# Tables of the means' turns read from SBUF, and their comparisons moved among the additions

## The reference

```python
# layer 0: messages weighted by an MLP of the edge attributes, summed at each src node
h = jax.nn.silu(edge_rbf @ W1 + b1)
aggregated = jax.ops.segment_sum(node_feats[col] * (h @ W2 + b2), row, num_segments=n_nodes)
x = _layernorm(x + (jnp.concatenate([node_feats @ Wself + bself, aggregated], -1) @ Wcat + bcat))
# layer 1: means over the neighbours in both directions, then a GRU cell
a_in  = _seg_mean((h @ W_in.T + b_in)[src], dst, N)
a_out = _seg_mean((h @ W_out.T + b_out)[dst], src, N)
x = _layernorm(x + _gru_cell(jnp.concatenate((a_in, a_out), 1), h, w_ih, w_hh, b_ih, b_hh))
```

## Time and profile before

| what | value |
|---|---|
| time, median of 3 runs | 7878.73 us (7873.51 to 7900.0) |
| profiled execution, its own time | 7875.48 us |
| its span, first to last instruction | 7873.8 us |
| busy share: PE, DVE, ACT, POOL | 57%, 56%, 11%, 63% |
| mean granted clock of PE | 0.708 of full |
| stage of the means, first to last addition | 3290.5 to 7527.1 us |

### The profile page before, as it was taken

One profiled execution on the slowest core, in us unless ns is written; L12 is line 12 of the kernel. 1 busy time (PEld: TensorE's weight loads), 2 busy tenths in 40 slices (PEclk: granted clock), 3 DMA queues, 4 the chain that ended last, 5 costly groups with the idle time before them and its releaser, 6 DMA issues.

```text
span 7873.8 us, 126494 instructions
## 1 busy us (share of the span) xinstructions
PE 4516.3 (57%) x27084; PEld 3894.4 (49%) x27084; DVE 4432.0 (56%) x16895; ACT 841.4 (11%) x1997; POOL 4968.8 (63%) x5292
## 2 busy tenths in 40 slices
PE   4999999999997888433333333332333333333378
PEld 3777877777777886333333323232232332332344
DVE  7666666666668883444444544445444544444455
ACT  1222222222220001000000000000000000000023
POOL 1777777777772110477777777777577777777710
PEclk7778778777878995566666666666666666666689
DMA  2333333333336772222222222222122222222222
GB/s 91 111 111 112 110 112 111 112 109 112 110 107 217 225 221 67 69 51 54 53 53 53 51 53 53 53 53 52 37 53 53 50 53 53 53 53 53 53 64 74
DMA packets 872793, 657.16 MB, mean 83 GB/s; under 512 B 564443, under 2 KB 760144, under 8 KB 872064
## 3 DMA queue, kind: packets, MB, share of 16 engines
q0 software_dynamic: 163968, 348.11, 15.1%
q1 hardware_dynamic: 641797, 242.70, 13.1%
q10 hardware_dynamic: 66944, 65.50, 2.7%
HBM read 504.82 MB, written 138.16 MB: 82 GB/s over the span
## 4 chain that ended last, share of the span: by engine, by line
PE 21%; DVEq 15%; DVE 14%; POOL 9%; issue 9%; DMA 1%; ACT 0%; POOLq 0%; SPq 0%; ACTq 0%
DVEq L350 12%; POOL arena L657 9%; PE bank L1668 8%; PE bank L1620 6%; DVE acc_a L1347 5%; DVE acc_b L1347 5%; DVE arena L1336 3%; DVEq L1347 2%; PE bank L1712 1%; DVEq L1336 1%; PE bank L1649 1%; PE bank L1713 1%; PE bank L1714 1%; PE bank L1639 1%; PE bank L1647 1%
## 5 line engine op out<-in xcount | busy, mean ns | idle before, releaser
L657 POOL DMA_INDIRECT arena<-x1d,edge x3328 | 3190.7, 959 | 1086.6 <-issue 1006.3
L1668 PE MATMUL bank<-arena 128*128 x7040 | 1314.0, 370 | 2874.8 <-DVE arena L1336 2786.8
L1668 PEld LDWEIGHTS bank<-arena 128*128 128x128 f32 x7040 | 1269.0, 283 | 2920.0 <-issue 2920.0
L618 POOL DMA_INDIRECT msgs<-arena x1664 | 1646.4, 989 | 716.3 <-issue 495.6
L1336 DVE TENSOR_SCALAR arena<-iota_row,arena,edge 128x128 f32<-128x128 f32 x3520 | 935.9, 365 | 1287.0 <-issue 1282.9
L1347 DVE TENSOR_TENSOR acc_a<-acc_a,bank 128x129 f32 x1760 | 510.3, 290 | 463.2 <-PE bank L1668 240.9
L1347 DVE TENSOR_TENSOR acc_b<-acc_b,bank 128x129 f32 x1760 | 510.3, 290 | 438.9 <-PE bank L1668 219.7
L1592 PE MATMUL bank<-arena 128*128 (+1 forms) x3328 | 618.3, 343 | 0.0
L1560 PE MATMUL bank<-arena 64*128 64x128 f32 x3328 | 606.8, 336 | 0.4 <-ACT arena L723 0.4
L1568 PE MATMUL bank<-w2s,acc_b 128*128 128x128 f32 x3328 | 581.8, 328 | 0.0
L1620 PE MATMUL bank<-arena 128*128 128x128 f32 x3712 | 504.5, 301 | 94.3 <-DVE arena L1173 94.1
(11 more groups left out here) (275 smaller groups left out, 4197.2 us busy)
## 6 DMA issues: line engine op xcount, KB each, us to landing
arena<-rows SPq DMA_DIRECT2D x208, 512.0 KB
arena<-msgs SPq DMA_DIRECT2D x464, 136.0 KB, 3.0
arena<-msgs ACTq DMA_DIRECT2D x464, 136.0 KB, 3.2
arena<-x1d,edge POOLq DMA_INDIRECT x3328, 2.5
msgs<-arena POOLq DMA_INDIRECT x1664
arena<-xwin SPq DMA_DIRECT2D x208, 64.0 KB
arena<-acc_a SPq DMA_DIRECT2D x28, 448.0 KB, 4.7
arena<-in_edge_attr_dram SPq DMA_DIRECT2D x207, 32.0 KB
```

The source lines that it names most:

```text
L618: pool.indirect_dma_start(msgs, bass.IndirectOffsetOnAxis(ap=pos[:, b, j:j + 1], axis=0), mrow[:, b, j, :], None).then_inc(scattered[b], 16)
L657: pool.indirect_dma_start(grow_t[:, sl, 0:D], None, x1d, bass.IndirectOffsetOnAxis(ap=edge2[:, odd * RING + sl, 1:2].bitcast(i32), axis=0) ...
L1668: last = mm(bank[q % 2 * 4 + k // 2][:, (k % 2) * 256:(k % 2) * 256 + CW], oh1[:, q % 2, k, :], grow[:, bass.ds(rows_at[q * TG + k], CW)], ...
```

## The change

The tables of the turns are still written to DRAM. SP now copies each turn's 32 values (128 bytes) into one of two slots in SBUF (`turntab`, in the memory of `tprod`, which the messages' stage used), when DVE has made the first comparisons of the turn that comes two turns earlier. DVE waits for the slot and loads its registers from there. SP's list loads are placed between these copies; in half 1 the first copy comes after the first 16 lists, of which the last eight come after the second table has landed.

On DVE a turn makes the eight comparisons of group 0; then, for each of the eight passes, one comparison of group 1 followed by one addition of group 0, the first addition waiting for PE's group 0; then it waits for PE's group 1 and adds eight. The loop over turns has two turns in its body. Two semaphores are merged into others (`w1_in` into `xcopy`, `dstq_in` into `count_in`, with the waits raised to match).

```diff
+        turntab = tprod[:, :, :].rearrange("p a b -> p (a b)")[0:1, 0:4 * NT].bitcast(i32).rearrange("p (s k) -> p s k", s=2)
...
+        turn_in = [sem(f"turn_in{i}") for i in range(2)]
...
@@ SP, lists and tables @@
-            for b in range(ahead, GL):
-                need(sp, s["sum1_ready"], max(2 * b - 17, 0))
-                list_load(0, b)
+            def turn_load(half, it):
+
+                first = half * V1 // TG + it * (NT // TG)
+                need(sp, s["oh1_ready"], first - 2 * (NT // TG) + 1)
+                sp.dma_start(turntab[:, it % 2, :], sumtab[half:half + 1, it, :]).then_inc(turn_in[it % 2], 16)
+
+            for it in range(IT1):
+                turn_load(0, it)
+                b = it + ahead - 10
+                if ahead <= b < GL:
+                    sp.wait_ge(s["sum1_ready"], 2 * b - 17)
+                    list_load(0, b)
             sp.wait_ge(s["dst_sorted"], 1)
-            for b in range(GL):
-                sp.wait_ge(s["sum1_ready"], min(191 + 2 * b, V1 // TG) if b < ahead else V1 // TG + 2 * b - 17)
+            for b in range(ahead):
+                sp.wait_ge(s["sum1_ready"], min(191 + 2 * b, V1 // TG))
                 if b == ahead // 2:
                     pair_table(1)
+                    for i in range(2):
+                        sp.wait_ge(pair_copied[i], 2 * 64 * (CHUNKS // 2))
                 list_load(1, b)
+            for it in range(IT1):
+                turn_load(1, it)
+                b = it + ahead - 10
+                if ahead <= b < GL:
+                    sp.wait_ge(s["sum1_ready"], V1 // TG + 2 * b - 17)
+                    list_load(1, b)
@@ DVE, one turn @@
-            def sums1(half, it, lists):
+            def sums1(half, it, lists, slot, loads, start=False):
...
-                regs, of = load_table(dve, "dve_sum", 2 * NT, sumtab[half:half + 1, bass.ds(it, 1), :].rearrange("o t k -> o (t k)"), [NB * CW] * NT + [2 * LISTS - 2] * NT)
+                dve.wait_ge(turn_in[slot], 16 * loads)
+                dve.nop(nofuse=True)
+                regs, of = load_table(dve, "dve_sum", 2 * NT, turntab[:, slot, :], [NB * CW] * NT + [2 * LISTS - 2] * NT)
...
-                def onehots1(q):
-                    need(dve, s["sum1_ready"], first + q - 1)
+                def onehot1(q, k):
+                    return v.tensor_scalar(oh1[:, q % 2, k, :], iota_row[:, :], blk1[:, bass.ds(it * NT + q * TG + k, 1)], edge2_f[:, bass.ds(key_at[q * TG + k], 1)], ALU.add, ALU.is_equal)
+
+                if half or not start:
+                    dve.wait_ge(s["sum1_ready"], first - 1)
+                for k in range(TG):
+                    last = onehot1(0, k)
+                last.then_inc(s["oh1_ready"], 1)
+                for q in range(turn):
+                    more = q < turn - 1
+                    if more and (half or not start):
+                        dve.wait_ge(s["sum1_ready"], first + q)
                     for k in range(TG):
-                        last = v.tensor_scalar(oh1[:, q % 2, k, :], iota_row[:, :], blk1[:, bass.ds(it * NT + q * TG + k, 1)], edge2_f[:, bass.ds(key_at[q * TG + k], 1)], ALU.add, ALU.is_equal)
-                    last.then_inc(s["oh1_ready"], 1)
-
-                onehots1(0)
-                for q in range(turn):
-                    if q < turn - 1:
-                        onehots1(q + 1)
-                    dve.wait_ge(s["sum1_ready"], first + q + 1)
-                    for k in range(TG):
-                        need(dve, s["add1_done"], v0 + it * NT + q * TG + k)
+                        if more:
+                            last = onehot1(q + 1, k)
+                            if k == TG - 1:
+                                last.then_inc(s["oh1_ready"], 1)
+                        if k == 0:
+                            dve.wait_ge(s["sum1_ready"], first + q + 1)
+                        if k or q or half or not start:
+                            dve.wait_ge(s["add1_done"], v0 + it * NT + q * TG + k)
                         a = acc[:, bass.ds(at[q * TG + k], CW)]
                         v.tensor_tensor(a, a, bank[q % 2 * 4 + k // 2][:, (k % 2) * 256:(k % 2) * 256 + CW], ALU.add).then_inc(s["add1_done"], 1)
@@ DVE, the loop of turns: two turns in a body @@
-                with dve.Fori(max(a, 1), min(b, GL)) as it:
-                    sums1(half, it, it + half * GL + 1)
+                with dve.Fori(max(a // 2, 1), min(b, GL) // 2) as c:
+                    for i in range(2):
+                        sums1(half, 2 * c + i, 2 * c + i + half * GL + 1, i, c + lead)
...
```

More of the change, by code:

```diff
@@ L306, in gnn_kernel @@
         g_out g_stats g_moments u_added u_moments u_kept g_mv u_inv g_inv aux_split xcopy pool_step gather_own upd_step
-        grow_ones tiles_in lists_in list_in dstq_in pair_sums pair_out count_in slow_total slow_start w1_in slow_pool lotab_out reg_done wide_in digits_read local_ready slow_blocks slow_counted
+        grow_ones tiles_in lists_in list_in pair_sums pair_out count_in slow_total slow_start  slow_pool lotab_out reg_done wide_in digits_read local_ready slow_blocks slow_counted
         slow_hist rows_float columns_ready columns_read blk0_copied totals_in totals_out base_in""".split()
@@ L376, in _ @@
             for j in range(TG):
-                sp.dma_start(w1pad[j * A:(j + 1) * A, j, :], W1).then_inc(s["w1_in"], 16)
+                sp.dma_start(w1pad[j * A:(j + 1) * A, j, :], W1).then_inc(s["xcopy"], 16)
             sp.wait_ge(s["prep_out"], 1)
@@ L397, in _ @@
             sp.wait_ge(s["lotab_out"], 48)
-            sp.wait_ge(s["xcopy"], 32)
+            sp.wait_ge(s["xcopy"], 16 * (2 + TG))
             sp.wait_ge(s["flag_ready"], 1)
@@ L518, in _ @@
                 sp.wait_ge(pair_copied[i], 64 * (CHUNKS // 2))
-            sp.dma_start(dst_q[0:EQ, 0:EC], dst.rearrange("(p c) -> p c", c=EC)).then_inc(s["dstq_in"], 16)
-            for b in range(ahead, GL):
-                need(sp, s["sum1_ready"], max(2 * b - 17, 0))
-                list_load(0, b)
+            sp.dma_start(dst_q[0:EQ, 0:EC], dst.rearrange("(p c) -> p c", c=EC)).then_inc(s["count_in"], 16)
+            def turn_load(half, it):
[8 more added lines that the diff above has]
+                    list_load(0, b)
             sp.wait_ge(s["dst_sorted"], 1)
-            for b in range(GL):
-                sp.wait_ge(s["sum1_ready"], min(191 + 2 * b, V1 // TG) if b < ahead else V1 // TG + 2 * b - 17)
+            for b in range(ahead):
+                sp.wait_ge(s["sum1_ready"], min(191 + 2 * b, V1 // TG))
                 if b == ahead // 2:
                     pair_table(1)
+                    for i in range(2):
+                        sp.wait_ge(pair_copied[i], 2 * 64 * (CHUNKS // 2))
                 list_load(1, b)
+            for it in range(IT1):
[4 more added lines that the diff above has]
+                    list_load(1, b)
             mean_rows = [a[:, 0:NB * CW].rearrange("p (n c) -> p n c", c=CW) for a in (acc_a, acc_b)]
@@ L988, in _ @@
             dve.wait_ge(s["lotab_out"], 48)
-            dve.wait_ge(s["xcopy"], 32)
+            dve.wait_ge(s["xcopy"], 16 * (2 + TG))
             cnt, start = kcol[0:NB, 0:1], kcol[0:NB, 2:3]
@@ L1361, in turns @@
             def turns(half, a, b):
+                lead = half * IT1 // 2 + 1
                 if a == 0:
-                    sums1(half, 0, half * GL + 1)
-                with dve.Fori(max(a, 1), min(b, GL)) as it:
-                    sums1(half, it, it + half * GL + 1)
+                    for i in range(2):
+                        sums1(half, i, i + half * GL + 1, i, lead, start=(i == 0))
+                with dve.Fori(max(a // 2, 1), min(b, GL) // 2) as c:
+                    for i in range(2):
+                        sums1(half, 2 * c + i, 2 * c + i + half * GL + 1, i, c + lead)
                 if b == IT1:
-                    with dve.Fori(GL, IT1) as it:
-                        sums1(half, it, half * GL + GL)
+                    with dve.Fori(GL // 2, IT1 // 2) as c:
+                        for i in range(2):
+                            sums1(half, 2 * c + i, half * GL + GL, i, c + lead)
             pair_table(0)
@@ L1372, in _ @@
             turns(0, 0, ITH)
-            dve.wait_ge(s["dstq_in"], 16)
+            dve.wait_ge(s["count_in"], 32)
             for c, shift, mask in ((0, 7 + LO.bit_length() - 1, None), (1, 7, LO - 1)):
@@ L1600, in _ @@
             pe.wait_ge(s["prepared"], 1)
-            pe.wait_ge(s["w1_in"], 16 * TG)
+            pe.wait_ge(s["xcopy"], 16 * (2 + TG))
             pe.wait_ge(s["aux_in"], 16 * 6)
```

## The result

The changed kernel takes 8053.82 us (median of 4 runs, 8049.06 to 8064.51) against 7885.47 us of the kernel before beside it: a ratio of 1.022, interval 1.0203 to 1.0236. It is slower, as forecast (8072 us). The profiled execution took 8064.51 us with a span of 8062.9.

What follows compares the result with a forecast made beforehand. A serial DVE-PE ring of 18.79 us a turn bounds, POOL nearly as slow. Turns +198, start of half 1 +14, start of half 0 -5, gather waits -10: +197 us on 7875.48, 8072 us; range 7860 to 8290.

Steps and rivals of the forecast that it cites:

- ring of links: DVE's serial chain with PE in one turn of the means stage: 19.69 us forecast against 18.79 before.
- Table load: DVE's idle time at a turn's start: 2.65 us from the slot instead of 5.87, 3.22 us saved per turn.
- Mixing: Additions of group 0 alternating with comparisons of group 1 on DVE: 0.47 us a pair, between 0.42 and 0.69.
- second rival: Mixing on DVE hides nothing: a pair costs 0.69 us, 1.32 us more per turn, 8360 us; chance 0.10.
- Second group: PE's second eight passes, now waited for by DVE: 3.92 us per turn, at the 1.2 GHz clock level.
- first rival: PE's second group runs at full clock: turn 17.94 us, POOL bounds, 7825 us, 0.6% faster; chance 0.10.
- The queue's order: DVE takes its queue strictly in order, so seven ready comparisons stand behind the wait for PE's first group.
- third rival: Written order does not bind DVE; comparisons run under PE as before: turn 15.57 us, POOL bounds, 7825 us; chance 0.03.
- start of half 1: First slot of the second half is requested only after eight lists on SP, so DVE starts later: +14 us.
- start of half 0: First load of 9.44 us becomes a landing of 2.2 us and a load of 2.1 us: -5 us.
- waits for late gathers (-10): Turns where PE's second group and DVE waited for a gather find POOL ahead: three such waits, -10 us.
- One sign: A mark to look for in the profile after: POOL waiting for PE for over 200 us in total.

Runs made afterwards that it cites:

- the ring alone: Kernel before, with tables loaded from the SBUF slots but all sixteen comparisons still ahead of the additions: 7830.15 us, ratio 0.9936.

## Why the prediction was right

The mechanism was the forecast one, and its ring of links holds link by link:

| link of a turn | predicted | measured, mean |
|---|---|---|
| idle time ahead of the comparisons | 2.65 | 2.52 |
| eight comparisons to PE's start | 2.37 | 2.40 |
| first group to the first addition | 3.92 | 3.93 |
| mixed stretch to PE's second start | 3.59 | 3.49 |
| second group to the next addition | 3.92 | 3.93 |
| last eight additions | 3.24 | 3.25 |
| turn (average, without the three that hold a pause) | 19.69 | 19.51 |

*Table load.* A load from the slot takes 2.10 us, as the load of the earlier stage did, and the idle time lies between the two ends that were named, 2.42 and 2.92. DVE waited for a slot's landing twice in all, at the start of each half, as forecast.

```profile
L352 DVEq TENSOR_LOAD <-tprod x220: 2097/2101/2243, 3300.8 to 7691.3; - x110
```

*Mixing.* Additions recur at 0.46 us (4771.78 to 4772.24), against the 0.47 taken. The second rival's 0.69 does not occur.

*Second group.* This was the new wait, and its price was right because the clock was low: 3.70 us on average. The first rival had the right price too: with the second group fast, the time was 7841 us, against the 7825 forecast for that case. The prediction's reason, that PE has stood still before the group, is only part of it. In 101 of the 220 turns the clock stood at 1.00 for some of the gap, where PE has nothing to do, and in 80 of these it was back at 0.50 when the second group began; in the other 119 it did not rise before the second group. The Trainium skill, "TensorE: Matmul & The Clock Gate", section "HAM oscillation — how this bites in real kernels", describes a kernel in which a wait between bursts throttles PE again, so that every burst starts cold; the trace agrees in the 80 turns, and in the 119 there was no faster clock to lose.

*The queue's order.* The third rival fell: the seven comparisons stood behind the wait of 4.01 us, the first of them until 4771.98. By the rule of the Trainium skill, "TensorE: Matmul & The Clock Gate", section "Architectural detail: the array is 16x 32x32, not 1x 128x128", they had to, and the trace agrees.

*Sizes that were off.* The average turn of before was 18.86 us and not the 18.79 of the turn that was read, and that of after 0.18 under the forecast: 0.65 us more per turn and not 0.90, 143 us and not 198. At the start of half 1 the pause grew by 14.8 us, forecast +14; the pause in which the means are formed by 3.4, which was not forecast: DVE's load lay hidden there before too (14.45 us between the turns in both kernels), so that turn gains nothing from the ring. At the start of half 0 the forecast was -5 and the trace has +2 from the clearing of `acc_b` to the first comparison (53.2 to 55.2 us): the term that failed is the landing, taken as 2.2 us from another DMA, where 9.30 were measured; the copy was issued behind the 830 KB transfer on SP, and without that it took 1.17. The waits for late gathers (-10) did go; they stand in the 18.86. With 143 + 14.8 + 3.4 + 2 us, 163 of the stage's 166.9 are accounted for. That the total, +197, came within 30 us is in part luck: the turns were put 55 us too high, and the terms outside them, with the -10 that the average turn already holds, 21 us too low. One sign was set too high: POOL was to wait for PE for over 200 us, and waited 171.3.

*POOL.* POOL takes over as soon as DVE gets faster, as the prediction has it, and this hid the ring's gain: 7830 us with the ring alone, and only with half of the gathers does its worth show.

## What to carry to other kernels

An engine that runs its queue in order pays for the place of a wait, not for its length alone: put everything that is ready ahead of it, and mix only what is left. Before an order is changed to hide one latency, list what the old order hid; here mixing saved some 1.6 us of DVE's time and laid bare one and a half bursts of PE. A part that gains is easily lost in a pair of edits: run each alone, and with the next bound taken away, to see what it is worth.

## What the runs showed of the hardware that was not expected

The time of the second group goes by degrees with the gap ahead of it: 3.70 us on average after a gap of 3.67 us in the changed kernel, 3.21 after 2.28 us with four comparisons ahead, and 2.35 with products of constants in the gap, while the first group took 3.73 to 3.74 in all three. The clock itself has only its two levels in these traces; what changes is in how many turns the group begins at 1.00 (21, 142 and 198 of 220), and whether the clock falls within it. A copy of 128 bytes landed after 9.30 us behind a transfer of 830 KB on the same queue, after 1.17 us without it.
